# Two blocks of attention and feed-forward on one core: query and key units of half heads, sixteen heads at a time

## What is computed

```python
xn = layernorm(x)                                   # block 0
q, k, v = split(xn @ qkv_w + qkv_b)                 # 32 heads of 16 features
q, k = rope(q), rope(k)     # x1, x2 = halves of 8: [x1*cos - x2*sin, x2*cos + x1*sin]
s = softmax(causal(q @ k.T / 4)) @ v @ out_w + out_b
g = silu((silu(xn @ W_gate.T) * (xn @ W_up.T)) @ W_down.T)
x = x + s * g
xn = layernorm(x)                                   # block 1
x = x + convolution_network(xn) * silu(ternary_ffn(xn))
```

## Time and profile before

| what | value |
|---|---|
| median of 3 runs | 640.55 us (639.74 to 642.76) |
| the profiled execution | 640.25 us, of which the span from the first to the last instruction is 638.3 us |
| busy share | PE 95%, DVE 60%, POOL 59%, ACT 43% |
| head of b = 0, start of the projections to first score | 14.3 to 39.3 us |
| slots and the rest of block 0, b = 0 | to 237.1 us |
| head of b = 1 | 237.1 to 261.7 us |
| slots and the rest of block 0, b = 1 | to about 452 us |
| block 1 | about 452 to 638 us |

### The profile page before, as it was taken

How to read it: one execution, slowest core, us unless ns; L and a number is a source line. 1 busy time by engine, 2 the same in 40 slices (tenths; PEclk the granted TensorE clock), 3 DMA queues, 4 the chain that set the end, 5 groups by cost and what they waited for, 6 DMA issues and landing times.

```text
span 638.3 us, 9817 instructions
## 1 busy us (share of the span) xinstructions
PE 603.8 (95%) x3348; PEld 417.5 (65%) x3348; DVE 381.9 (60%) x920; ACT 276.3 (43%) x440; POOL 377.6 (59%) x596
## 2 busy tenths in 40 slices
PE   3997999999999999989999999999999999999996
PEld 2864565666657878655656665578888676767664
DVE  4956867666524587596686664264986251525257
ACT  3513554655653533055555556436222344332432
POOL 5875766655443577677565554345988676641264
PEclk9998999999999999999999999999999999999999
DMA  9768675754441235758558644644440000000002
GB/s 287 233 209 289 192 197 142 222 125 112 93 133 50 85 97 173 195 166 269 144 151 266 186 111 115 257 165 126 138 175 1 0 1 1 1 1 0 1 30 103
DMA packets 60370, 83.63 MB, mean 131 GB/s; under 512 B 17937, under 2 KB 26769, under 8 KB 60321
## 3 DMA queue, kind: packets, MB, share of 16 engines
q1 hardware_dynamic: 57392, 73.70, 39.6%
q10 hardware_dynamic: 2928, 9.31, 4.0%
HBM read 65.17 MB, written 26.99 MB: 144 GB/s over the span
## 4 chain that ended last, share of the span: by engine, by line
PE 79%; DVE 6%; DMA 5%; POOL 4%; SPq 2%; issue 2%; ACT 2%; POOLq 0%; DVEq 0%; ACTq 0%
PE proj_ps L932 9%; PE ctx_ps L1090 6%; PE proj_ps L934 6%; PE proj_ps L933 6%; PE score_ps L962 5%; PE proj_ps L1138 3%; PE proj_ps L1139 3%; PE scoreT_ps L971 3%; PE score_ps L932 3%; PE score_ps L934 2%; PE score_ps L933 2%; DMA k_st<-rows 2%; PE scoreT_ps L932 2%; PE scoreT_ps L934 2%; PE scoreT_ps L933 2%
## 5 line engine op out<-in xcount | busy, mean ns | idle before, releaser
L751 POOL TENSOR_TENSOR w_lo<-raw,w_hi 128x512 fp32r<-128x512 f32 x98 | 132.6, 1358 | 67.9 <-ACT w_hi L1293 61.2
L1479 DVE CUSTOM_DVE_ANT_0 score_ps<-score_ps,causal 128x512 f32<-128x512 f32 (+3 forms) x256 | 119.9, 516 | 60.6 <-PE score_ps L962 60.2
L1337 ACT ACTIVATE probs_T<-scoreT_ps 128x1024 f32<-128x1024 f32 (+1 forms) x96 | 84.9, 884 | 82.2 <-PE scoreT_ps L971 81.5
L932 PE MATMUL proj_ps<-xn_hi,w_hi 128*128 128x512 f32 x224 | 99.8, 446 | 0.3 <-POOL w_lo L751 0.3
L934 PE MATMUL proj_ps<-xn_lo,w_hi 128*128 128x512 f32 x224 | 88.4, 395 | 0.0
L933 PE MATMUL proj_ps<-xn_hi,w_lo 128*128 128x512 f32 x224 | 88.3, 394 | 0.0
L749 POOL TENSOR_SCALAR w_hi<-raw 128x512 fp32r<-128x512 f32 x50 | 31.2, 625 | 51.8 <-PE proj_ps L934 48.9
L962 PE MATMUL score_ps<-k_st,q_st 50*128 50x512 f32 (+3 forms) x256 | 44.6, 385 | 14.1 <-DVE row_max L1479 8.7
L932 PEld LDWEIGHTS proj_ps<-xn_hi,w_hi 128*128 128x128 f32 x224 | 42.0, 188 | 24.4 <-issue 9.6
L962 PEld LDWEIGHTS score_ps<-k_st,q_st 50*128 50x128 f32 x256 | 21.7, 186 | 54.8 <-issue 25.5
L785 POOL TENSOR_SCALAR_AFFINE_SELECT probs_T<-probs_T 128x256 f32<-128x256 f32 x128 | 50.5, 414 | 11.4 <-ACT probs_T L1337 11.4
(11 more groups left out here) (306 smaller groups left out, 1309.9 us busy)
## 6 DMA issues: line engine op xcount, KB each, us to landing
raw<-w SPq DMA_DIRECT2D x98, 256.0 KB, 3.0
rows<-rows_hi SPq DMA_DIRECT2D x32, 256.0 KB, 3.8
arranged<-tern SPq DMA_DIRECT2D x96, 85.0 KB
q_st<-rows SPq DMA_DIRECT2D x32, 200.0 KB
k_st<-rows SPq DMA_DIRECT2D x32, 200.0 KB
rows<-rows_lo SPq DMA_DIRECT2D x16, 256.0 KB, 4.5
gate_w<-arranged ACTq DMA_DIRECT2D x4, 704.0 KB, 6.8
up_w<-arranged ACTq DMA_DIRECT2D x4, 704.0 KB, 7.8
```

The source lines that it names most:

```text
L751: nc.gpsimd.tensor_tensor(w_lo[n % SPLIT][:, :], raw[n % RAW][:, :], F32(w_hi[n % SPLIT][:, :]), ALU.subtract).then_inc(unit_ready, 1)
L932: nc.tensor.matmul(acc, lh, rh, start=first, stop=False)
L1337: nc.scalar.activation(probs_T[gp % 4][:, c:c + 2 * w].rearrange("p (h c) -> p h c", h=2), scoreT_ps[:, :, 0:w], ACT.Exp, scale=0.25).then ...
L1479: m = nc.vector.tensor_tensor_reduce(out=block, in0=block, in1=causal[:, S - w:], scale=1.0, scalar=-3e38, op0=ALU.add, op1=ALU.max, accum ...
```

## The change

Query and key units are cut the other way. A unit now holds one half (8 of the 16 features) of sixteen heads, so a chunk of sixteen heads needs four units: query first and second half, key first and second half. Both halves of a head then sit in the same partition of two units, and each unit needs only two products and one sum or difference. `U0`..`U3` are units 0 to 3, the values move to 4 to 7, the second chunk's units are 9, 11, 13, 15 in place of six units between 9 and 19. In front of slot 0 PE now projects four units, the values and two units (8 and 9) in place of two, the values and three. POOL's `rope_lo` and ACT's `rope_hi` for U0 and U1 go between the splits of units 5 to 7; `U2` and `U3` have row buffers of their own in the space of `probs_T0`. SP writes the rows of U0 and U1 after loads 10 and 11, of U2 and U3 before load 12, then reads groups 0 and 1. The `tern` writes go between the loads of slot 0. The sum for the ternary thresholds moves from `proj_ps[1]` to `first_ps[0]`.

```diff
@@ constants and the order of the slots
-Q_UNIT, K_UNIT, V_UNIT = (0, 9, 12, 18), (1, 10, 13, 19), 2
-FFN_UNIT = [6, 7, 8, 11, 14, 15, 16, 17] + list(range(20, 34))
-IN_FRONT = 3 * KC
-FILL = 6
+QK_UNIT, V_UNIT = ((0, 1, 2, 3), (9, 11, 13, 15)), 4
+FFN_UNIT = [8, 10, 12, 14] + list(range(16, 34))
+CHUNKS = 2
+IN_FRONT = 2 * KC
+FILL = 8
...
+def turned_in(s):
+    return [u for u in sorted(QK_OF) if u >= FILL and unit_slot(upper(u)) + 2 + QK_OF[u][2] == s]
...
 def rest_in_slot(s):
-    return [u for u in sorted(QK_OF) if u >= FILL and unit_slot(u) + 3 == s]
+    return turned_in(s - 1)
...
 def written_in(s):
-    return [u for u in sorted(QK_OF) if u >= FILL and unit_slot(u) + 4 == s]
+    return turned_in(s - 2)
...
 def read_in(s):
-    return next((g for g in range(1, GROUPS) if (1 if g == 1 else max(6 * g - 6, unit_slot(K_UNIT[g // 2]) + 6)) == s), None)
+    return next((g for g in range(2, GROUPS) if max(6 * g - 6, unit_slot(QK_UNIT[g // 4][3]) + 7) == s), None)
...
-HI_BY_ACT = FILL + 3
-RAW_HEAD = 12
+HI_BY_ACT = FILL + 1
+RAW_HEAD = 13
@@ buffers
+    rows_hi += [sb(f"rows_hi{2 + t}", [P, S], f32r, offset=o_pt0 + 4096 * t) for t in range(2)]
+    rows_lo += [sb(f"rows_lo{2 + t}", [P, S], f32r, offset=o_pt0 + 4096 * t + 2048) for t in range(2)]
...
-    rows_d = [[nc.dram_tensor(f"rows{t}{b}", (KC, 8, HEAD_ROWS, S), f32, kind="Internal").ap() for t in range(2)] for b in range(B)]
+    rows_d = [[nc.dram_tensor(f"rows{t}{b}", (CHUNKS, 16, HEAD_ROWS, S), f32, kind="Internal").ap() for t in range(2)] for b in range(B)]
...
-    def written(b, t, c, x):
-        return rows_d[b][t][c][:, 2 + D * x:2 + D * x + D, :].rearrange("h d s -> d h s")
...
+    def written(b, t, c, h, x):
+        first = 2 + D * x + D // 2 * h
+        return rows_d[b][t][c][:, first:first + D // 2, :].rearrange("h d s -> d h s")
@@ the queue of SP
-                c, h = g // 2, 4 * (g % 2)
-                sp.wait_ge(rows_stored, 96 * (KC * b + c + 1))
+                c, h = g // 4, 4 * (g % 4)
+                sp.wait_ge(rows_stored, 96 * (KC * b + 2 * c + 2))
...
                 for u in range(RAW if b else 0, RAW_HEAD):
+                    if u == 12:
+                        write_rows(b, QK_UNIT[0][2])
+                        write_rows(b, QK_UNIT[0][3])
                     load(b, u)
...
-                    if u == 9:
-                        write_rows(b, Q_UNIT[0])
-                        write_rows(b, K_UNIT[0])
+                    if u in (10, 11):
+                        write_rows(b, QK_UNIT[0][u - 10])
                 read_rows(b, 0)
+                read_rows(b, 1)
@@ the head on POOL
+                    if u in (5, 6):
+                        rope_lo(b, QK_UNIT[0][u - 5])
+                rope_lo(b, QK_UNIT[0][2])
+                rope_lo(b, QK_UNIT[0][3])
@@ the head on PE
-                for u in (Q_UNIT[0], K_UNIT[0]):
+                for u in QK_UNIT[0]:
+                    if b and job(u) == 2:
+                        pe.wait_ge(combined, 2 * NT * (b - 1) + NT)
@@ the ropes on DVE
-                nc.vector.scalar_tensor_tensor(out=by_sin[t][0:64, :], in0=ps[64:128, :], scalar=bias[64:128], in1=rope_sin[64:128, :],
-                                               op0=ALU.add, op1=ALU.mult).then_inc(sin_half, 1)
-                nc.vector.scalar_tensor_tensor(out=by_sin[t][64:128, :], in0=ps[0:64, :], scalar=bias[0:64], in1=rope_sin[0:64, :],
+                nc.vector.scalar_tensor_tensor(out=by_sin[h][:, :], in0=ps[:, :], scalar=bias, in1=rope_sin[:, :],
                                                op0=ALU.add, op1=ALU.mult).then_inc(proj_free, 1)
...
-                nc.vector.tensor_tensor(turned_rows[t][:, :], by_cos[t][:, :], by_sin[t][:, :], ALU.add).then_inc(turned_ready, 1)
+                nc.vector.tensor_tensor(turned_rows[h][:, :], by_cos[h][:, :], by_sin[1 - h][:, :],
+                                        (ALU.subtract, ALU.add)[h]).then_inc(turned_ready, 1)
...
             def first_ropes(b):
 
-                for u in (Q_UNIT[0], K_UNIT[0]):
-                    rope_first(b, u)
-                    rope_second(b, u)
+                for t in range(2):
+                    for u in QK_UNIT[0][2 * t:2 * t + 2]:
+                        rope_first(b, u)
+                    for u in QK_UNIT[0][2 * t:2 * t + 2]:
+                        rope_second(b, u)
```

More of the change, by code:

```diff
@@ L644, in write_rows @@
             def write_rows(b, u):
-                t, c = QK_OF[u]
+                c, t, h = QK_OF[u]
                 r = rope_job(b, u)
@@ L702, in _ @@
                         read_rows(b, read_in(s))
-                    for u in raw_in_slot(s):
+                    for x, u in enumerate(raw_in_slot(s)):
                         load(b, u)
+                        if b == 0 and s == 0 and 1 <= x <= 3:
+                            sp.wait_ge(wp_ready, x)
+                            for half, src in enumerate((tern_pos[x - 1], tern_neg[x - 1])):
+                                sp.dma_start(tern_d[x - 1][half].rearrange("(p n) -> p n", p=P), F32(src[:, :])).then_inc(tern_stored, 16)
                     if b == 0 and s == 3:
@@ L754, in rope_lo @@
             def rope_lo(b, u):
-                t, r = QK_OF[u][0], rope_job(b, u)
+                t, r, n = QK_OF[u][2], rope_job(b, u), rows_buffer(u)
                 pool.wait_ge(rows_hi_ready, r + 1)
-                if r >= 2:
+                if r >= 2 and n < 2:
                     pool.wait_ge(rows_stored, 96 * (r // 2))
-                nc.gpsimd.tensor_tensor(rows_lo[t][:, :], turned_rows[t][:, :], F32(rows_hi[t][:, :]), ALU.subtract).then_inc(rows_lo_ready, 1)
+                nc.gpsimd.tensor_tensor(rows_lo[n][:, :], turned_rows[t][:, :], F32(rows_hi[n][:, :]), ALU.subtract).then_inc(rows_lo_ready, 1)
             def join_maxima(b, j):
@@ L1020, in _ @@
                     pe.wait_ge(asum_ready, 3)
-                    nc.tensor.matmul(proj_ps[1][:, 0:3], V[:, 0, 0:P], abs_sums[:, :], start=True, stop=True).then_inc(tot_ready, 1)
-                else:
-                    pe.wait_ge(combined, 2 * NT * (b - 1) + NT)
+                    nc.tensor.matmul(first_ps[0][:, 0:3], V[:, 0, 0:P], abs_sums[:, :], start=True, stop=True).then_inc(tot_ready, 1)
                 for kc in range(KC):
@@ L1265, in rope_hi @@
             def rope_hi(b, u):
-                t, r = QK_OF[u][0], rope_job(b, u)
+                t, r = QK_OF[u][2], rope_job(b, u)
                 act.wait_ge(turned_ready, r + 1)
-                if r >= 2:
+                if r >= 2 and rows_buffer(u) < 2:
                     act.wait_ge(rows_stored, 96 * (r // 2))
-                nc.scalar.activation(rows_hi[t][:, :], turned_rows[t][:, :], ACT.Copy).then_inc(rows_hi_ready, 1)
+                nc.scalar.activation(rows_hi[rows_buffer(u)][:, :], turned_rows[t][:, :], ACT.Copy).then_inc(rows_hi_ready, 1)
             def load_rows(w, T, done, chunks):
@@ L1310, in _ @@
             for b in range(B):
-                for u in range(5 if b else RAW, FILL):
+                for u in range(5 if b else RAW, HI_BY_ACT):
                     split_hi(UNITS * b + u)
[L1313 to L1317, removed]
+                    if u in (5, 6):
+                        rope_hi(b, QK_UNIT[0][u - 5])
+                rope_hi(b, QK_UNIT[0][2])
+                rope_hi(b, QK_UNIT[0][3])
                 act.wait_ge(ones_set, 2 + b)
@@ L1578, in _ @@
                 for u in units_after(0):
-                    ffn_out(b, u)
+                    ffn_out(b, u) if u in FFN_OF else rope_first(b, u)
                 for s in range(SLOTS):
@@ L1809, in constants @@
     cos, sin = np.cos(ang).astype(np.float32), np.sin(ang).astype(np.float32)
-    rope = np.stack([np.repeat(np.concatenate([cos, cos], 1).T, 8, 0), np.repeat(np.concatenate([sin, -sin], 1).T, 8, 0)])
-    edges = np.zeros((2, KC, 8, 2, S), np.float32)
+    rope = np.stack([np.repeat(w.T, 16, 0) for w in (cos, sin)])
+    edges = np.zeros((2, CHUNKS, 16, 2, S), np.float32)
     edges[1] = -1.0
```

66 lines of the change are left out of this document (31 added, 35 removed).

## The result

The changed kernel takes **665.24 us** (median of 4 runs, 663.02 to 666.42) against 641.65 us for the kernel before in the same comparison: ratio 1.0384, 95% interval 1.0352 to 1.0416. It is slower, as forecast, but by 23.6 us where 11 were forecast, and 665.24 lies outside the range of 640 to 657. The profiled execution took 666.42 us with a span of 664.4, so 26.1 us more span than before, and that is the amount to be explained. It is 2.5 us more than the medians differ by, since the profiled execution is the slowest of the four.

The account below looks back on a forecast made before the run. PE, busy 95% of the span, was taken as the bound. From 640.25 us, less 4.87 and 1.72 (group 1) and 7.0 (DVE), plus 21.2 (late group 0) and 3.4 (low clock), came 651.3 us; range 640 to 657.

Parts of the forecast that it names:

- Eight engines, the main term: Row writes before slot 0 use eight DMA engines, 1.37 us each; PE waits 10.5 and 10.7 us for group 0.
- The first rival: Row writes before slot 0 stay on 16 engines, 0.8 us each; waits of 3.9 and 4.1 us, 638.1 us; chance 0.18.
- Group 1 read in the head: Reading group 1 before slot 0 removes its two slot 6 waits, 4.87 us, and 1.72 us of low clock.
- The late read spreads: Loads behind group 0's read make POOL late for the first maxima; some 2 us per sequence, 655 us; chance 0.15.
- The low clock: PE runs partly at 1.2 GHz behind the new wait before slot 0 of each sequence; 1.72 us added twice.
- DVE's relief: Two rope multiplications in place of three shorten PE's waits for row maxima; 7.0 us gained, ends 4 and 8.7.
- the forecast's lower end of 4 us: Least gain on row maxima waits, if a rope sum, an output and 512-wide maxima meet in slot 15.
- More units in front, at nothing: Two more units before slot 0, one less behind the values: first score 2.7 us later, but no cost.
- ACT's order changes: ACT's copies of V need 2.5 us and have two units' 5.4 us, so its new order costs nothing.
- the other zeros: Slower second-chunk writes, SP held at group 4's read and separate row buffers were each taken to cost nothing.
- The landing time of the writes: A sign: time to landing of the `rows` writes far above 3.8 us.

Follow-up runs that it names:

- e1: The changed kernel with head-major columns and rope tables, so row writes have sixteen heads outermost in place of 8; 648.53 us, ratio 1.0150.
- e2: The kernel before with row writes sent with eight heads outermost in place of 16 features, rows permuted; 650.21 us, ratio 1.0182.
- e4: The kernel before with group 1 read right behind group 0 in front of slot 0, in place of in slot 1; 642.04 us, ratio 1.0039.
- f4: f2 with a third full-width product on DVE in each rope, into a tile nothing reads; 645.22 us, ratio 1.0076.
- f5: The kernel before with two rope products in place of three, leaving out the exchange of a head's halves; 638.20 us, ratio 0.9969.
- g3: f3 with f5's edit, two rope products in place of three; 637.82 us, ratio 0.9968.
- f3: e4 with fourteen loads ahead of the reads in place of twelve; 643.51 us, ratio 1.0061.
- f2: f1 with twelve triples in front of slot 0 in place of eight; 640.78 us, ratio 1.0011.
- e3: The changed kernel with 15 loads ahead of the reads in place of 13; 660.73 us, ratio 1.0330.
- f1: The changed kernel with the edits of e1 and e3 together; 646.40 us, ratio 1.0099.
- g1: f2 with group 0 read ahead of loads 12 to 14 in place of behind them; 646.53 us, ratio 1.0082.
- g2: g1 with sixteen triples in front of slot 0 in place of twelve; 644.36 us, ratio 1.0060.

## Why the forecast was right in its sign and wrong in its size

**Eight engines, the main term: right.** A share near 0.5 and under 200 GB/s was named; 0.53 and 204 were measured, so 25.5 GB/s for each of eight engines, and 1.28 us a write where 1.37 was taken. The packets in the traces rule out that all sixteen were at work for half the time: from 38 to 40 us 8 to 10 packets were under way together in the changed kernel, from 34 to 36 us 15 to 19 in e1. By the rule of the Trainium skill that the forecast cited (page "DMA: Bandwidth & Descriptors", section "Why a DMA increments its semaphore by 16 and not by 1"), eight engines were to be expected; e1 and e2 agree with it. The forecast had the new waits at 10.5 and 10.7 us; they were 11.80 and 11.24. From the first row write (29.25 us) to the issue of the read (50.11) 20.9 us passed, forecast 19.8, and the read took 7.0 us to 57.12, forecast 6.5. The write started 3 us later than the 26.2 us of the forecast, but PE was as much later itself (45.3 against 42.0), so that cancelled. The term was 21.2 us and is 23.0. The first rival fell with the share; its numbers came true in e1, where its condition was made true.

**Group 1 read in the head: right in the line, wrong in the sum.** Both stack waits are gone, 4.87 us. But "its two waits go" misreads one of them. Slot 6 of the second sequence, where group 1 is first used, starts at 277.03 us; PE waited there for row maxima, and SP had issued group 1's read 11 us earlier. Timelines of PE and of SP's queue, kernel before:

```profile
277.03 0.50 PE L962 MATMUL score_ps<-k_st,q_st 50*128 50x512 f32 x2 [0.90 <-DVE row_max L1479]
```

```profile
265.62 0.71 SPq L665 DMA_DIRECT2D q_st<-rows  x2
```

The wait at 292.82 us is at slot 12, for group 2, and the read issued at 286.25 us, from which the forecast timed a read at 6.5 us, is group 2's. That wait went since group 2 now lies in the first sixteen heads, whose rows are stored before slot 0. And the waits were booked as a gain, where e4 shows that on the kernel before group 1's is none: the reads stand ahead of the loads, and 4.2 us of `max_cols` waits come for it.

**The late read spreads: the rival that held beside the forecast.** It was given 0.15 as an alternative, with "1 to 2 us of margin" for POOL and "some 2 us per sequence" as its price. It cost 3.24 and 2.50 us, and its own low clock behind. The failed step is that margin: it counted the bytes, and left out POOL's work behind them. The bytes were right: from the issue of the read (50.11 us) to the first of the three splits (63.91) 13.8 us passed, and the forecast's 4.6 MB at 329 GB/s take 14.0. But three units of 1.9 us each (0.63 and 1.27, split in turn) then came before the first join at 69.74, 5.8 us in all, and a margin of 1 to 2 us has no room for them. Nothing kept this rival from holding together with the forecast; at its own price the sum would have been 655.

**The low clock: counted behind two waits, and there were four.** "I add 1.72 us twice", for the two k_st waits. The windows of the changed kernel give 1.9 and 1.7 us lost behind these (3.88 and 3.41 us of work at 0.50), so this price was about right, and 1.7 us behind each `max_cols` wait (1 x 0.38 + 2 x 0.50 + 2 x 0.16 for the first; 2 x 0.17 + 2 x 0.50 + 4 x 0.09 for the second), for which the sum had nothing. That is 7.0 us, less the 1.72 of before: +5.3, where the forecast's sum had +1.7.

**DVE's relief: 7.0 taken, 4.4 came.** Six waits remain, 4.3 us. The forecast had each rope's wait shrink by 0.75 us of DVE work. But 4.0 of the 4.3 us stand in two places of each sequence: 0.76 us behind a rope's two products (87.93 us) and 1.23 us behind a rope sum and an output (104.85 us). Timeline of DVE, changed kernel, ahead of the second:

```profile
101.03 1.63 DVE L1563 TENSOR_TENSOR turned_rows<-by_cos,by_sin 128x512 f32<-128x512 f32 x1
102.58 0.67 DVE L1538 SCALAR_TENSOR_TENSOR gate_silu<-gate_tanh,proj_ps 128x512 f32<-128x512 f32 x1
103.17 0.55 DVE L1499 CUSTOM_DVE_ANT_0 score_ps<-score_ps,causal 128x384 f32<-128x384 f32 x1
```

A rope sum, an output and then the maxima: a pile-up of the kind behind the forecast's lower end of 4 us. The sum alone took 1.63 us here, where the sixteen have a mean of 0.94. Rope multiplications are 32 in place of 48, as said. f4 (4.4 us for giving the load back), f5 (2.0) and g3 (5.7 over f3, by medians) put the relief between 2 and 6 us; what decides within that is open. 7.2 us of waits taken away gave 2.0 us in f5, and 7.8 gave 5.7 in g3 (2.9 by the spans).

**More units in front, at nothing: not refuted, not settled.** f2 shows that the twelve triples of before are worth 5.6 us over eight once k_st is late; 2.5 of them are shorter k_st waits. The forecast's two more units in front and one less behind were a net of one; as the k_st term was made against PE's own readiness, this is in the 23.0 us. For "ACT's order changes" and the other zeros no line stands out: the small waits are 1.1 us less together. The landing time of the writes, named as a sign, is not given by the profile after.

**The sum again**, from 638.3 us of span: k_st +18.1 (forecast +16.3), `max_cols` +5.7 (0), clock +5.3 (+1.7), row maxima -4.4 (-7.0) make 24.7. The start (+1.1), the rest of PE's busy time (+1.4) and the small waits (-1.1) make the 26.1. Against the forecast's +11.0 that is 15.1 more: 5.7 from `max_cols`, 3.6 from the clock, 2.6 from DVE, 1.8 from k_st, 1.4 from the rest. The upper end of 657 had room for any one of these; all of them came, on the same side.

## What to carry to other kernels

Look at the outermost dimension of every DRAM access when rows are cut in another way: the same bytes in the same number of transfers went at 204 or 333 GB/s by that order alone, 15 to 17 us of this kernel. When a transfer becomes late, follow its queue behind it to the engine that runs dry, with the work that this engine must still do, and add that wait and the slower clock behind it; a rival that does not exclude the forecast belongs in the sum. And a wait taken away is not a gain of its own length: a part can come back at the next wait, as 2.6 of 7.8 us did in g3. Before a wait is priced, count the slots to see what it is for: two waits on the same tiles were here for different groups.

## What had not been expected of the hardware

Eight busy DMA engines moved 25.5 GB/s each (204 over 8), sixteen busy with the same writes 20.8 (333 over 16): half the engines give six tenths of the rate.

In the profiled execution of the changed kernel the first eleven matmuls of the head start some 0.427 us apart, in e1's 0.227, while the granted clock is given as 1.00 in both. 0.427 us is also the spacing of such matmuls behind the k_st wait, where the granted clock is 0.50 (58.43, 58.86, 59.28 us). Timeline of PE, changed kernel, then e1:

```profile
16.41 0.63 PE L956 MATMUL score_ps<-xn_lo,w_hi 128*128 128x512 f32 x1
16.84 0.63 PE L954 MATMUL score_ps<-xn_hi,w_hi 128*128 128x512 f32 x1
```

```profile
16.21 0.39 PE L956 MATMUL score_ps<-xn_lo,w_hi 128*128 128x512 f32 x1
16.44 0.39 PE L954 MATMUL score_ps<-xn_hi,w_hi 128*128 128x512 f32 x1
```

That is 2.2 us (11 x 0.2). Seven of the fourteen profiled executions have this spacing in the first nine to eleven matmuls (the changed kernel, e3, f1, f2, f5, g1, g2). The kernel before has not, nor has f4, which differs from f2 in one product on DVE. So up to 2.2 of the 6.7 us of PE's longer busy time may be the execution's and not the change's; with the 5.3 us of the clock that makes 7.5 us, 0.8 more than the busy time shows. Whether the slow start varies from run to run or goes with a kernel was not tried.
